# An LSTM recurrence in which the low half of h comes from a two-column scan, with both tanh results side by side in SBUF

## What is computed

```python
def step(carry, xp):
    h, c = carry
    gates = xp + h @ W_hh.T
    i, f, g, o = jnp.split(gates, 4, axis=-1)
    c = jax.nn.sigmoid(f) * c + jax.nn.sigmoid(i) * jnp.tanh(g)
    h = jax.nn.sigmoid(o) * jnp.tanh(c)
    return ((h, c), h)
_, hs = jax.lax.scan(step, (h0, c0), jnp.swapaxes(x_proj, 0, 1))
```

## Time and profile before

| what | value |
|---|---|
| median of 3 runs | 7796.72 us (7796.51 to 7797.44) |
| the profiled execution's own time | 7795.31 us |
| its span in the trace | 7793.5 us |
| PE busy | 4576.0 us (59% of the span) |
| DVE busy | 5392.0 us (69%) |
| ACT busy | 2826.5 us (36%) |
| granted TensorE clock, mean | 0.591 |

### The profile page before, as it was taken

How to read it: one execution, slowest core, us unless ns; L and a number is a source line. 1 busy time by engine, 2 the same in 40 slices (tenths; PEclk the granted TensorE clock), 3 DMA queues, 4 the chain that set the end, 5 groups by cost and what they waited for, 6 DMA issues and landing times. The chain is left out here.

```text
span 7793.5 us, 179150 instructions
## 1 busy us (share of the span) xinstructions
PE 4576.0 (59%) x57602; PEld 3112.0 (40%) x57632; DVE 5392.0 (69%) x30722; ACT 2826.5 (36%) x14714; POOL 217.1 (3%) x504
## 2 busy tenths in 40 slices
PE   4555555555555555555555555555545958899799
PEld 3444444444444444444444444444433422244344
DVE  7666666666666666666666666666646669999544
ACT  3333333333333333333333333333321000289333
POOL 0000000000000000000000000000000020000111
PEclk6555555555555555555555555555556976699899
DMA  1000000000000000000000000000001810000000
GB/s 45 14 13 14 13 14 14 12 14 13 14 14 12 14 12 14 13 13 14 13 14 13 14 14 12 14 12 14 4 2 66 280 49 0 2 1 1 24 4 5
DMA packets 93263, 164.30 MB, mean 21 GB/s; under 512 B 8711, under 2 KB 23087, under 8 KB 92337
## 3 DMA queue, kind: packets, MB, share of 16 engines
q1 hardware_dynamic: 89009, 150.47, 6.1%
q10 hardware_dynamic: 2816, 2.10, 0.1%
q0 software_dynamic: 512, 0.53, 0.0%
HBM read 146.25 MB, written 2.10 MB: 19 GB/s over the span
## 5 line engine op out<-in xcount | busy, mean ns | idle before, releaser
L431 PE MATMUL lstm_gates<-lstm_h_parts,lstm_wrec 128*128 128x1 f16 x36864 | 2075.8, 170 | 2821.3 <-DVE lstm_h_parts L576 2813.0
L431 PEld LDWEIGHTS lstm_gates<-lstm_h_parts,lstm_wrec 128*128 128x128 f16 x36864 | 1618.8, 107 | 3423.6 <-DVE lstm_h_parts L576 3412.5
L487 ACT ACTIVATE lstm_tanhs<-lstm_gates 128x3 f32<-128x3 f32 x4096 | 708.0, 173 | 2723.0 <-PE lstm_gates L431 2722.8
L431 PE MATMUL lstm_gate_o<-lstm_h_parts,lstm_wrec 128*128 128x1 f16 x12288 | 1440.7, 165 | 0.0
L576 DVE SCALAR_TENSOR_TENSOR lstm_h_parts<-lstm_tanh_o,lstm_c_pair 128x1 f16<-128x1 f32 x4096 | 646.4, 158 | 908.7 <-ACT lstm_c_pair L493 908.7
L571 DVE SCALAR_TENSOR_TENSOR lstm_terms<-lstm_tanhs 128x2 f32<-128x2 f32 x4096 | 659.3, 161 | 765.9 <-ACT lstm_tanhs L487 546.0
L595 DVE RECIPROCAL lstm_rec<-lstm_dist 128x52 f32<-128x52 f32 (+1 forms) x2560 | 1171.8, 462 | 4.2 <-issue 4.2
L493 ACT ACTIVATE lstm_c_pair<-lstm_c_pair 128x1 f32<-128x1 f32 x4096 | 639.0, 156 | 954.3 <-DVE lstm_terms L571 954.3
L431 PEld LDWEIGHTS lstm_gate_o<-lstm_h_parts,lstm_wrec 128*128 128x128 f16 x12288 | 961.1, 104 | 0.0
L454 PE MATMUL lstm_acc<-msg,lstm_wt 128*128 128x128 f32 x2048 | 780.3, 488 | 37.9 <-DVE lstm_wt L603 37.9
L582 DVE TENSOR_TENSOR lstm_h_parts<-hid_t,lstm_h_parts 128x1 f16<-128x1 f32 x4096 | 668.3, 163 | 182.1 <-DVE hid_t L578 13.0
(11 more groups left out here) (261 smaller groups left out, 4585.1 us busy)
## 6 DMA issues: line engine op xcount, KB each, us to landing
lstm_ring<-in_adj SPq DMA_DIRECT2D x256, 256.0 KB, 2.7
gnn_ring<-in_adj SPq DMA_DIRECT2D x64, 1024.0 KB, 5.3
w<-in_w SPq DMA_DIRECT2D x2, 1364.0 KB, 9.9
heads_cos<-in_cos SPq DMA_DIRECT2D x8, 256.0 KB, 3.1
heads_sin<-in_sin SPq DMA_DIRECT2D x8, 256.0 KB, 3.6
qs<-heads_q_high SPq DMA_DIRECT2D x64, 32.0 KB, 2.3
out<-x SPq DMA_DIRECT2D x8, 256.0 KB, 2.3
ks<-heads_k_high ACTq DMA_DIRECT2D x16, 64.0 KB, 2.4
```

The lines of the kernel that those rows point to most:

```text
L431: return nc.tensor.matmul(o, wrec[:, w, g, :], h_parts[:, (n - 1) % NH, k:k + 1], start=False, stop=True, skip_group_check=True)
L487: nc.scalar.activation(tanhs[:, 0:3], gates[t % 2][:, i, :], ACT.Tanh, scale=unscale).then_inc(tanhs_ready, 1)
```

## The change

The two tanh results lie side by side in one SBUF tile `tanh_pair`, tanh_o in column 0 and tanh_c in column 1, so ACT writes `tanh_c` into SBUF where it wrote PSUM. A ring slot of `h_parts` has five float16 columns: column 1 holds -1 from the start, column 2 the high half, column 4 the low half. The low half comes from one instruction, a scan over two columns whose running value starts at 1, is multiplied by `tanh_pair` and lessened by columns 1 and 2: first tanh_o * 1 - (-1), then tanh_c * (tanh_o + 1) - high. It needs the high half and not the full product, so the full product moves behind it. Since `tanh_pair` is now read by that full product, ACT waits for the full product of the step before (`full_ready`) ahead of the next tanh_o. On PE the two products of the high half for the output gate move behind the low half's three products for the other gates.

```diff
-        tanh_o = ph.sb("tanh_o", [P, 1])
-        c_pair = ph.ps("c_pair", [P, 2])
-        c_twice, tanh_c = c_pair[:, 0:1], c_pair[:, 1:2]
+        c_sum, tanh_pair = ph.ps("c_sum", [P, 1]), ph.sb("tanh_pair", [P, 2])
+        c_twice, tanh_o, tanh_c = c_sum[:, :], tanh_pair[:, 0:1], tanh_pair[:, 1:2]
-        h_parts = ph.sb("h_parts", [P, NH, 2], F16)
+        h_parts = ph.sb("h_parts", [P, NH, 5], F16)
...
                     for g in range(3):
                         part(w, g, 0)
-                for w in range(2):
-                    part(w, 3, 0)
                 pe.wait_ge(low_ready, n + 1)
                 part(0, 0, 1)
                 part(0, 1, 1)
                 part(0, 2, 1).then_inc(gates_ready, 1)
+                for w in range(2):
+                    part(w, 3, 0)
                 part(0, 3, 1).then_inc(gate_o_ready, 1)
...
                 act.wait_ge(gate_o_ready, n + 1)
-                nc.scalar.activation(tanh_o[:, :], gate_o[t % 2][:, i:i + 1], ACT.Tanh,
+                if n >= 1:
+                    act.wait_ge(full_ready, n)
+                nc.scalar.activation(tanh_o, gate_o[t % 2][:, i:i + 1], ACT.Tanh,
                                      scale=unscale).then_inc(tanh_o_ready, 1)
...
+            s.done(nc.vector.memset(h_parts[:, :, :], -1.0))
...
-                nc.vector.scalar_tensor_tensor(out=h_parts[:, n % NH, 0:1], in0=tanh_o[:, :], scalar=1.0,
-                                               in1=tanh_c, op0=ALU.add, op1=ALU.mult).then_inc(high_ready, 1)
-                nc.vector.scalar_tensor_tensor(out=T.hid_t[:, n:n + 1], in0=tanh_o[:, :], scalar=1.0,
-                                               in1=tanh_c, op0=ALU.add, op1=ALU.mult).then_inc(full_ready, 1)
-                dve.wait_ge(full_ready, n + 1)
+                nc.vector.scalar_tensor_tensor(out=h[:, 2:3], in0=tanh_o, scalar=1.0, in1=tanh_c,
+                                               op0=ALU.add, op1=ALU.mult).then_inc(high_ready, 1)
                 dve.wait_ge(high_ready, n + 2)
-                nc.vector.tensor_tensor(h_parts[:, n % NH, 1:2], T.hid_t[:, n:n + 1], h_parts[:, n % NH, 0:1],
-                                        ALU.subtract).then_inc(low_ready, 1)
+                nc.vector.tensor_tensor_scan(out=h[:, 3:5], data0=tanh_pair[:, :], data1=h[:, 1:3], initial=1.0,
+                                             op0=ALU.mult, op1=ALU.subtract).then_inc(low_ready, 1)
+                nc.vector.scalar_tensor_tensor(out=T.hid_t[:, n:n + 1], in0=tanh_o, scalar=1.0, in1=tanh_c,
+                                               op0=ALU.add, op1=ALU.mult).then_inc(full_ready, 1)
```

More of the change, by code:

```diff
@@ L430, in part @@
                     o = gate_o[t % 2][:, i:i + 1] if g == 3 else gates[t % 2][:, i, g:g + 1]
-                    return nc.tensor.matmul(o, wrec[:, w, g, :], h_parts[:, (n - 1) % NH, k:k + 1], start=False,
+                    return nc.tensor.matmul(o, wrec[:, w, g, :], h_parts[:, (n - 1) % NH, 2 * k + 2:2 * k + 3], start=False,
                                             stop=True, skip_group_check=True)
@@ L562, in _ @@
             s.done(nc.vector.tensor_tensor(wrec[:, 1, :, :], wtmp[:, :, :], wrec[:, 0, :, :], ALU.subtract))
+            s.done(nc.vector.memset(h_parts[:, :, :], -1.0))
             nc.vector.memset(c_twice, 0.0).then_inc(weights_ready, 1)
             nc.vector.memset(tanhs[:, 3:4], 0.0).then_inc(c_kept, 1)
-            nc.vector.memset(h_parts[:, NH - 1, 0:1], 0.0).then_inc(high_ready, 1)
-            nc.vector.memset(h_parts[:, NH - 1, 1:2], 0.0).then_inc(low_ready, 1)
+            nc.vector.memset(h_parts[:, NH - 1, 2:3], 0.0).then_inc(high_ready, 1)
+            nc.vector.memset(h_parts[:, NH - 1, 4:5], 0.0).then_inc(low_ready, 1)
             def step(n):
+                h = h_parts[:, n % NH, :]
                 dve.wait_ge(tanhs_ready, n + 1)
```

## The result

The changed kernel takes 7579.98 us (median of 4 runs, 7575.54 to 7583.11) against 7796.72 before: a ratio of 0.972, 95% interval 0.9705 to 0.9738. That is 217 us less; the forecast was 164 us less, 7633 us, and the range 7530 to 7764. The profiled execution took 7575.54 us with a span of 7573.7 us.

A forecast was written before the change was run, and what follows sets the result against it. A chain of latencies, not a full engine, was taken to bound each step: 423 - (163 + 42 + 165) - 13 = 40 ns less, times 4096 is 164 us, giving 7633 us; range of 8 in 10: 7530 to 7764.

The forecast's parts named there:

- The handover: On DVE, from one instruction to the next before the low half: 42 ns, as between full product and subtraction before.
- high, full, low: DVE's chain before the change: the low half starts just after the full product ends, and everything behind hangs on it.
- The start of the chain, before: From the high half's start to the low half's start in the kernel before: 260 ns, plus 163 for the low half.
- The scan: The two-column scan on DVE that gives the low half: 165 ns, lower bound 160, ordinary range up to 185.
- the rival of a fixed price: The scan on DVE has a fixed price of its own, with 60 ns more making 7879 us; chance 0.10.
- SBUF: tanh_c into SBUF adds 13 ns on ACT (bounds 0 and 17); the high half adds 5, at most 13.
- Output gate last: PE's output-gate products moved last add nothing on the path; without the move the gain would just about be reached.
- ACT's new wait and the full product behind the scan: ACT's wait ahead of tanh_o is always over; the full product behind DVE's scan is off the path: no cost.

The follow-up runs named there:

- runs on waits: Kernel before without the subtraction's wait for the high half: 7752.59 us; changed kernel with a second wait before the scan: 7599.38 us, or 7878.03 us in the other order.
- run with one wait: Kernel before, with the subtraction that gives the low half waiting for the full product alone, its wait for the high half left out: 7752.59 us, ratio 0.9944.
- run on widths: Changed kernel plus scans of 2 to 258 columns behind the recurrence, each followed by a two-input instruction of the same width: 7577.8 us in a single run.
- run with a second wait: Changed kernel with a wait for the sum for c added before the scan: 7599.38 us written after the high half's wait, 7878.03 us written before it.

## Why the prediction was right, and where its sizes were off

The direction and the range held, and so did the chain but for what set the start of the low half. Its terms, in ns a step, against the means over all 4096 steps of the two traces:

| term | forecast | measured |
|---|---|---|
| from start of high half to end of low half, before | 423 | 265.2 + 163.2 = 428.4 |
| the same after: high half + handover + scan | 163 + 42 + 165 = 370 | 162.5 + 34.3 + 163.4 = 360.2 |
| taken out there | 53 | 68.2 |
| tanh of c into SBUF | 13 | 15.2 |
| a step shorter by | 40 | 53.9 |

- **The handover was mis-sized, and its reading was wrong.** It took the 42 ns between full product and subtraction as the price of a handover on DVE and carried it over. The runs on waits show that 34 is the price, and that those 42 were no handover from the full product at all, but the tail of a late wait in front. That is 8 of the 15 ns missing from the DVE term, 33 us.
- **The gain hung on a wait that the sum did not count.** The chain "high, full, low" as it stands ahead of the prediction leaves out the late wait, which ended 7 ns after the full product let go. Dropping that wait alone gives 44 of the 217 us; the scan with such a wait in front gives none (7878 against 7876 us). That the edit took the full product and the second wait away together is what made the gain, and the prediction reasoned for the first alone: on this point it was lucky.
- **The start of the chain, before.** One step of the timeline, with two decimals, gave 260 ns; the mean is 265, of which 3 ns are the 33 stalled steps that no single step shows. That is 5 ns, 20 us, and the run with one wait shows that the stalls go with the second wait.
- **The scan** was put at 165 and takes 163; the run on widths shows the fixed part equal to a two-input instruction's and 2.08 ns a column, so the rival of a fixed price is out. The Trainium skill's rule of half throughput ("DVE: opcode table, instruction layouts, handler registers and perf-mode slots", Datapath and trigger behaviour) agrees with 2.08 against 1.04.
- **SBUF** costs 15 and 5 ns, inside the bounds of 17 and 13, and the run that changes only that gives the 79 us back. The Trainium skill's warning ("ScalarE: Activation LUTs", Step-by-step: what each stage is for) has the right sign. The 42 ns that the Trainium skill, "Perfetto Trace Analysis", Optimizing Scalar/DVE Operations, gives between ScalarE's two memories do not show for a change of the destination alone: here it is 15.
- **Output gate last** costs nothing on the path: tanh_o is 0.42 us early. That the move would be needed was read rightly from the spacing of the loads, but too gently: the prediction said that without it the gain would just be reached, and the run shows 67 us lost.
- **ACT's new wait and the full product behind the scan** cost nothing on the path, as said; the sum for c starts 34 ns after the tanh of the gates in both kernels (mean). The new wait does stall ACT ahead of tanh_o in 38 steps, 6.9 us in all, which the 0.42 us to spare cover.

In all, 13.9 ns a step were missed (15.2 on DVE, less 2.2 on ACT, and 0.9 in the handovers of the rest of the chain), 57 us; the two times are 53 apart.

What the stalled steps wait for can be read a little further from the traces. Counted along DVE's own stream of instructions, wait instructions included, all 33 stalled subtractions of the kernel before stand at the same place in a block of 128 instructions, and every subtraction at that place stalls. Of the 34 stalled scans in each run with a second wait, 33 stand there and one stands one place on. From the end of the wait instruction to the start of the next it is 395 to 397 ns in the median in these kernels. ACT's 38 stalls ahead of tanh_o, also behind a wait instruction, fall on the same place of ACT's stream. Where no wait instruction stands in front, in the changed kernel, 30 scans stand at that place and 29 of them start after the usual 34 ns. This points to the supply of instructions, which a wait instruction lays bare; that reading is not tested by any run.

## What to carry to other kernels

In a recurrence, read one step's timeline as a chain and ask of every instruction on it which of its inputs comes last; a value that is only stored can stand behind the one that is waited for, and a scan over two columns did two dependent operations at the price of one instruction here. When that frees the path, look at once at what the next engine has queued in between: the reordering on PE was worth nothing before and 67 us after. Where an instruction needs two semaphores, look whether one of them is needless beside the other, and see to it that the one released last is not the one in front.

## What the runs showed of the hardware

- On DVE an instruction that waits by itself starts 34 ns after the end of the DVE instruction it waits for. Behind a separate wait instruction that is released late it starts 103 to 104 ns after it: 279 us between the two runs that differ in the order of two lines alone. A separate wait that is long over costs no handover, but brought back 34 stalls of some 0.3 us.
- The stalls behind a wait instruction come at one place in every 128 instructions of the engine's stream: 33 of 33 on DVE in the kernel before, 33 of 34 in each run with a second wait, 38 of 38 on ACT in the changed kernel.
- A scan in float32 costs 2.08 ns a column, against 1.04 for a two-input instruction, and the same fixed time; it takes 162 ns at two columns.
- The tanh of one column takes 156 ns into PSUM and 171 into SBUF; a two-input instruction takes 158 with one factor in PSUM and 163 with both in SBUF.
- Two float16 results written two columns apart take 165 ns, side by side 161.
